# A two-layer recurrent kernel on Trainium2: the first attention gates all its batches in its first half and routes in its third and fifth batch

## The chip, the core and the metric

The kernel runs as one program on one core of a Trainium2 chip. A core has a matrix engine (TensorE, in the rows PE for its multiplications and PEld for its weight loads), a vector engine (VectorE, DVE), a scalar engine (ScalarE, ACT), a general engine (GpSimd, POOL), and SyncE (SP), which here only starts DMAs. The engines run their own instruction streams and meet by semaphores. The metric is the device time of one execution in microseconds (us); the median of three runs of the kernel before is 748.44 us (747.85 to 749.85).

## What is computed

The input x has 8 batches of 512 tokens with 128 features, all float32. Two layers follow each other; in each, a normalised x goes through an attention s and a gated feed-forward part g, and x + s * silu(g) goes on.

```python
xn = _layernorm(x)
s = _L0_attn_ref(xn, W, b)              # causal attention, one head of 128, 512 x 512 scores for each batch
g = _silu(_L0_ffn_ref(xn, ...))         # below
x = x + s * g
xn = _layernorm(x)
s = _L1_attn_ref(xn, Mq, Mk, Mv)        # 8 heads of 64
g = _silu(_L1_ffn_ref(xn, ...))         # top 1 of 8 experts
x = x + s * g
```

```python
def _L0_ffn_ref(x, ...):
    xn = _layernorm(x, ln_g, ln_b)      # a second normalisation, with its own scale and shift
    abel = gelu(xn @ aw1 + ab1) @ aw2 + ab2
    logits = xn @ gate_w + gate_b       # 6 experts
    tw, ti = top_k(logits, 2)           # each token goes to its 2 best experts
    ... nonabel = (weighted sum of the 2 experts' outputs) @ expm(gens[0]) @ ... @ expm(gens[3])
    gate = sigmoid(concat(abel, nonabel) @ gc_w + gc_b)
    return x + abel * (1 - gate) + nonabel * gate
```

## The kernel before, in words

The program has these stages, one after the other:

1. The **first attention** (functions `batch`, L500 on TensorE, L635 on ScalarE, L800 on VectorE), batch by batch, eight times. A batch is 4 tiles of 128 tokens. Everything in it is written out by hand: each engine has one fixed order, with semaphore waits between them. The batch makes q, k and v from `xT` (L515, L517, L521), then for each of 4 query tiles: scores (L528), the largest of each row (L822), the exponential (L646), the turned exponentials (L535, copied by L829), the product with v (L545).
2. The **experts of layer 0**: 74 blocks of 128 rows (two halves of 37), each fetched from a table in DRAM (`x_half`), turned (L1023), sent up (L1033), through a gelu (L1125), down (L1043), and stored (L1358) to `y_half`. Half 0 holds the rows of batches 1 to 4, half 1 those of batches 5 to 8.
3. The dense part of layer 0 and the mixing, while POOL gathers the experts' rows back (L974).
4. Layer 1, attention and experts, to the end of the program.

Beside each batch of the first attention, the engines do other work of layer 0:

- **Normalisation.** VectorE takes mean and variance of a batch (`statistics`, L252), POOL makes the two scales from them (`scales`, L325: six small operations), VectorE writes the normalised tiles (`norm`, L675), POOL multiplies them by the second scale (L365, into `xh`, a part of `pool_xy`). TensorE turns both (`turn_xs` L422, `turn_xh` L429), ScalarE stores them as `xT` and `xn2T`.
- **Gate.** TensorE multiplies `xn2T` by the gate weights (`gate`, L484), VectorE stores the logits (`store_gate`, L704). Batch k prepares batch k + 1: its norm, its turns, its gate.
- **Routing.** After four gated batches VectorE picks each token's two experts (`picks`), TensorE counts (`ranks`), VectorE makes the slots (`offsets`, `first_blocks`, `slots`). This stands in batch 4 and batch 8 (`routes`, L832).
- **Scatters.** POOL writes each tile of `xh` to the rows of `x_half` that the slots name: two indirect DMAs for each of 32 tiles, each followed by a small clear (`spacer`, L350) that it waits for. The order on POOL is fixed: 8 scatters beside each of the preparations of batches 6, 7 and 8, the rest of half 0 after them, half 1 after batch 8's slots, then four additions of a bias (`add_bias`, L340).
- **Rounds.** The exponentials of the four generator matrices take 20 rounds (`exp_round` L436, `store_round` L683): 12 Taylor steps, one turning, 4 squarings (16 matrix instructions in place of 8), 3 products. Two stand in each of batches 1 to 7 and six in batch 8. In batch 8 the expert weights are turned as well (`turn_weights`), and after it they are multiplied by the product of the exponentials (L599, L605). The experts can't start before that (`w_ok`, L1029 and L1212).

## Time and profile before

| what | value |
|---|---|
| median of 3 runs | 748.44 us |
| the profiled execution, its own time | 754.12 us |
| its span, first to last instruction | 752.4 us |
| busy: PE, DVE, POOL, ACT | 641.5, 514.8, 445.5, 397.5 us |
| mean granted clock of TensorE | 0.954 of full |
| first attention, from the first q (L515) to the last product with v | 12.3 to 147.1 us |
| first expert block's first multiplication (L1033) | 158.86 us |

A row of the trace has the start and the length of an instruction or of a merged group in us, then the engine, the line of the kernel, the operation, what it writes and reads, and in brackets how long the engine stood idle before it and what ended that. A row of the windows gives a stretch, its length, the busy time of each engine in it, the granted clock of TensorE (1.00 is 2.4 GHz, 0.50 is 1.2 GHz), the mean share of the DMA engines, and GB/s. A busy TensorE is not TensorE at its peak. Durations come from one execution.

### The profile page before, as it was taken

To read this page: it belongs to the slowest core of one execution; us is meant where nothing else is said; L and a number is where in the kernel's file an instruction comes from. 1 tells how busy PE (TensorE), PEld (TensorE's weight loads), DVE (VectorE), ACT (ScalarE), POOL (GpSimd) and SP (SyncE) were. 2 spreads that over 40 slices of the span, in tenths; PEclk is the share of its full clock that TensorE was granted. 3 is DMA by queue.
4 is the path that set the end of the run, shared out by engine and by line. 5 is a ranking of instruction groups with operands and counts; after the bars stand their busy time and mean duration, and the time that the engine had idled before them with its cause. 6 is when DMAs were issued, how large, how long until landed. Compare 5 with 4: busy or idle time off the path is not lost.

```text
span 752.4 us, 19550 instructions
## 1 busy us (share of the span) xinstructions
PE 641.5 (85%) x6221; PEld 453.7 (60%) x6222; DVE 514.8 (68%) x1349; ACT 397.5 (53%) x1102; POOL 445.5 (59%) x651
## 2 busy tenths in 40 slices
PE   4996869588588888895679999998999999999993
PEld 3775657477587666674425555555999844454442
DVE  5787853947776635898488788786444476777784
ACT  2542442234244344775137767775444376777794
POOL 7441798489818879975016666423333167767692
PEclk9998998979999999997599999999999999999997
DMA  9992001126457631110000000000222101111110
GB/s 255 277 306 79 24 30 40 39 70 138 92 100 137 129 78 35 33 25 15 29 4 25 29 23 26 24 2 13 64 69 70 54 23 37 31 30 30 29 44 15
DMA packets 69466, 48.34 MB, mean 64 GB/s; under 512 B 8011, under 2 KB 63750, under 8 KB 69382
## 3 DMA queue, kind: packets, MB, share of 16 engines
q1 hardware_dynamic: 62332, 34.09, 17.4%
q0 software_dynamic: 6144, 12.63, 7.0%
q8 instruction: 47, 0.77, 0.4%
q10 hardware_dynamic: 906, 0.55, 0.3%
q14 instruction: 37, 0.30, 0.1%
HBM read 24.00 MB, written 23.24 MB: 63 GB/s over the span
## 4 chain that ended last, share of the span: by engine, by line
PE 43%; POOL 21%; issue 15%; DVE 12%; ACT 3%; DMA 3%; SPq 1%; DVEq 1%; POOLq 0%; ACTq 0%
PE bank L1657 9%; PE bank L1616 5%; PE bank L1709 5%; PE bank L1718 4%; POOL pool_xy L974 4%; PE bank L1642 4%; POOL vs L1567 3%; PE bank L1043 3%; PE bank L1033 3%; DMA xg<-x_half 2%; POOL x_half L354 2%; POOL spacer L969 2%; POOL xn_all L1546 2%; ACT pb L1777 1%; PE bank L1023 1%
## 5 line engine op out<-in xcount | busy, mean ns | idle before, releaser
L1777 ACT ACTIVATE pb<-bank,nmx 128x512 f32<-128x512 f32 x256 | 173.0, 689 | 67.0 <-DVE nmx L1908 66.6
L1908 DVE TENSOR_REDUCE nmx<-bank 128x2 f32<-128x1024 f32 x128 | 154.8, 1215 | 6.7 <-PE bank L1657 6.0
L1567 POOL TENSOR_TENSOR vs<-vt,rz 128x256 f32<-128x256 f32 x128 | 78.4, 615 | 118.4 <-DVE rz L1884 114.7
L1657 PE MATMUL bank<-qk 64*128 64x512 f32 x512 | 131.4, 623 | 7.8 <-ACT pb L1777 5.6
L1657 PEld LDWEIGHTS bank<-qk 64*128 64x128 f32 x512 | 42.6, 185 | 63.2 <-ACT pb L1777 32.3
L1125 ACT ACTIVATE turns<-bank,cols 128x128 f32<-128x128 f32 x148 | 46.2, 363 | 65.1 <-PE bank L1033 34.7
L1642 PEld LDWEIGHTS bank<-pb,vs 128*32 128x32 f32 x2048 | 54.2, 110 | 38.0 <-issue 22.4
L354 POOL DMA_INDIRECT x_half<-pool_xy,slot x64 | 62.5, 977 | 19.7 <-issue 10.5
L1642 PE MATMUL bank<-pb,vs 128*32 128x128 f32 x2048 | 69.7, 275 | 2.5 <-POOL vs L1567 2.2
L1777 ACT ACTIVATION_READ_ACCUMULATOR pb<-bank,nmx 128x1 f32 x256 | 53.0, 207 | 0.0
L1596 POOL COPY xn_all<-w 128x512 f32 x39 | 23.9, 613 | 47.8 <-PE bank L1709 47.8
L1033 PE MATMUL bank<-turns 128*128 128x128 f32 x296 | 49.8, 293 | 0.3 <-ACT turns L1125 0.3
L1043 PE MATMUL bank<-w_e,turns 128*128 x296 | 47.3, 284 | 0.8 <-issue 0.8
L1616 PE MATMUL bank<-xn2T,mq 128*32 128x256 f32 x512 | 42.0, 390 | 4.3 <-DVE qk L1860 2.2
L1918 DVE TENSOR_SCALAR xn_all<-bank,cols 128x128 f32<-128x128 f32 x78 | 23.8, 347 | 30.7 <-PE bank L1709 30.7
L974 POOL DMA_INDIRECT yg_first<-y_half,slot x32 | 31.1, 970 | 23.0 <-DMA y_half<-ys 17.8
L1078 PEld LDWEIGHTS bank<-w_a,hid 128*128 128x128 f32 x256 | 33.9, 196 | 16.8 <-issue 12.5
L1023 PE MATMUL bank<-ident,xg 128*128 128x128 f32 x74 | 23.2, 314 | 23.9 <-issue 8.8
L1709 PE MATMUL bank<-xn_all 128*128 128x128 f32 x312 | 43.0, 283 | 0.4 <-ACT xn_all L1787 0.4
L1043 PEld LDWEIGHTS bank<-w_e,turns 128*128 128x128 f32 x296 | 41.2, 201 | 1.0 <-issue 1.0
L1616 PE MATMUL bank<-xn2T,mk 128*32 128x256 f32 x512 | 41.4, 383 | 0.1
L1718 PE MATMUL bank<-w,xn_all 128*128 x312 | 41.4, 276 | 0.1
(254 smaller groups left out, 1387.0 us busy)
## 6 DMA issues: line engine op xcount, KB each, us to landing
y_half<-ys SPq DMA_DIRECT2D x74, 64.5 KB
x_half<-zero SPq DMA_DIRECT2D x2, 2368.0 KB, 21.2
xg<-x_half SPq DMA_DIRECT2D x74, 64.0 KB
x_sorted<-zero SPq DMA_DIRECT2D x1, 2496.0 KB, 19.0
xn_all<-x_sorted SPq DMA_DIRECT2D x39, 64.0 KB, 1.8
y_sorted<-xn_all SPq DMA_DIRECT2D x39, 64.0 KB, 1.6
x_all<-in_L_attn_x_dram SPq DMA_DIRECT2D x8, 256.0 KB, 6.2
w<-in_L_ffn_W_dram SPq DMA_DIRECT2D x1, 2048.0 KB, 11.4
```

The costliest lines, as they stand in the source:

```text
L354: pool.indirect_dma_start(out=x_half[g // NTH], out_offset=bass.IndirectOffsetOnAxis(ap=slot_w[:, g:g + 1], axis=0), in_=xh[:, g, :], in_o ...
L974: pool.indirect_dma_start(out=yg_half[h][:, g % NTH, w, :], out_offset=None, in_=y_half[h], in_offset=bass.IndirectOffsetOnAxis(ap=slot_w[ ...
L1033: mm = pe.matmul(psum[k % 2][:, c * P:(c + 1) * P], wst0[k % NW][:, c * P:(c + 1) * P], xgT0[k % 2][:, :], start=True, stop=True)
L1043: mm = pe.matmul(psum[MBANK[k % 2]][:, 0:DX], hT0[k % NW][:, c * P:(c + 1) * P], w_e2[:, bass.ds(e * EC + c, 1), :].rearrange("p a d -> p ...
L1567: pool.tensor_tensor(vs[s][:, :, :], vt[bt % 2][:, n // 2 % TT, :, :].rearrange("p j d -> p (j d)") .unsqueeze(1).broadcast_to([P, 2, D]), ...
L1616: mm = pe.matmul(bank[j * 32:(j + 1) * 32, i * TH:(i + 1) * TH], w[:, g * KS + j % 2 * 32:g * KS + j % 2 * 32 + 32], xn2T[:, bt * T + j // ...
L1642: mm = pe.matmul(bank[c * 2 * VD:(c + 1) * 2 * VD, at:at + P], vs[k % SLOTS][:, ab, c * 2 * VD:(c + 1) * 2 * VD], pb[k % SLOTS * 2 + ab][: ...
L1657: mm = pe.matmul(psum[score_banks(k) + ab], qk[bt % 2][half, 1, h, 2 * m:2 * m + 2, :].rearrange("p a k -> p (a k)"), qk[bt % 2][half, 0, ...
L1709: mm = pe.matmul(up_part(par, c), wst[par][:, c * P:(c + 1) * P], xgT[par][:, :], start=True, stop=True)
L1718: mm = pe.matmul(psum[(5, 6)[par]][:, 0:D], hT[par][:, c * P:(c + 1) * P], w_2[:, bass.ds(e * HC + c, 1), :].rearrange("p a d -> p (a d)") ...
L1777: act.activation(pb[s + ab][:, :], psum[score_banks(k) + ab], ACT.Exp, bias=nmx[:, s + ab:s + ab + 1], scale=1.0, accum_out=zz[:, s + ab:s ...
L1908: dve.tensor_reduce(nmx[:, s:s + 2], banks[:, score_banks(k):score_banks(k) + 2, :], AX.X, ALU.max, negate=True).then_inc(n_mx, 1)
```

## The change

- **All batches are gated in the first four.** Batch k (k = 1 to 4) now turns `xh` of batches 2k and 2k + 1 and gates batches 2k - 1 and 2k. VectorE's statistics of all batches move to batches 1 to 3, POOL makes all scales by then, and the normalised tiles of batches 3 to 8 are written by ScalarE (`norm`, a scale and a shift, the shift being made by POOL in two more small operations) and not by VectorE.
- **Routing stands in batches 3 and 5**, cut into parts between the steps of the attention: first pick at the batch's start, the other picks after the second and the third tile, the offsets at its end, the slots at the start of the batch behind it.
- **Scatters**: all 64 follow each other on POOL, with their small clears, once the scales and the rows of all batches are done. Each half waits for its own clearing of `x_half`; the clearing of half 0 is issued ahead of the late weights. The four bias additions still stand behind the last scatter.
- **Rounds**: two in batches 1 to 4, then three in each of batches 5 to 8. The turning of the expert weights moves to batches 6, 7 and 8 and its copies to ScalarE; half of the multiplications of the weights moves in front of batch 8's last product.

On POOL in the second half of the first attention stands before (`pool_xy<-xn_all` is a batch's rows by the second scale, `x_half` the scatter, `spacer` its clear; batch 8's preparation, between scatters):

```order
L350 MEMSET spacer 128x384
L354 DMA x_half<-pool_xy,slot 4736x128
L350 MEMSET spacer 128x384
L365 TENSOR_TENSOR pool_xy<-xn_all,rs 128x128 x4
L354 DMA x_half<-pool_xy,slot 4736x128
L350 MEMSET spacer 128x384
```

and now, where batches 7 and 8 are prepared in the first half (`xn_all<-xn_all,ab_bc` is a bias addition):

```order
L359 TENSOR_TENSOR pool_xy<-xn_all,rs 128x128 x4
L366 TENSOR_TENSOR xn_all<-xn_all,ab_bc 128x512
L359 TENSOR_TENSOR pool_xy<-xn_all,rs 128x128 x4
L366 TENSOR_TENSOR xn_all<-xn_all,ab_bc 128x512
L376 DMA x_half<-pool_xy,slot 4736x128
L372 MEMSET spacer 128x384
```

The rows of all batches now stand ahead of the first scatter.

On TensorE in batch 7 stood before (`ident,pool_xy` is the turning of `xh`, `ident,pr` that of the exponentials):

```order
L535 MATMUL bank<-ident,pr 128x128
L528 MATMUL bank<-kT,qT 128x384
L433 MATMUL bank<-ident,pool_xy 128x128 x4
L535 MATMUL bank<-ident,pr 128x128 x2
L545 MATMUL bank<-va,prT 128x128
L528 MATMUL bank<-kT,qT 128x512
```

and now:

```order
L563 MATMUL bank<-ident,pr 128x128
L556 MATMUL bank<-kT,qT 128x384
L563 MATMUL bank<-ident,pr 128x128 x2
L457 MATMUL bank<-gE,gET 128x128 x4
L459 MATMUL bank<-gET,gE 128x128 x4
L486 MATMUL bank<-ident,w_e 128x128 x4
L573 MATMUL bank<-va,prT 128x128
```

The turning of `xh` is gone from it, and a squaring (L457, L459) and a turning of weights (L486) came in.

At the end of batch 8, TensorE had:

```order
L545 MATMUL bank<-va,prT 128x128 x4
L599 MATMUL bank<-rotx,w_e2T 128x129 x12
L605 MATMUL bank<-rotx,eb2T 128x129 x6
L1014 UNCONDITIONAL_BRANCH
```

and has now:

```order
L497 MATMUL bank<-rotx,w_e2T 128x129 x6
L573 MATMUL bank<-va,prT 128x128 x4
L506 MATMUL bank<-rotx,eb2T 128x129 x6
L497 MATMUL bank<-rotx,w_e2T 128x129 x6
L1067 UNCONDITIONAL_BRANCH
```

Six of the twelve multiplications of weights moved ahead of the last product with v.

The diff, cut to its core:

```diff
 # POOL
-            def scales(bt):
+            def scales(j):
...
+                if j > 1:
+                    step(pool.tensor_tensor(nb, mean, r1, ALU.mult))
+                    pool.tensor_scalar(nb, nb, -1.0, None, ALU.mult).then_inc(nb_ok, 1)
...
             scales(0)
+            scale_rows(0)
+            pool.memset(zero[:, :], 0.0).then_inc(t_z, 1)
+            scales(1)
+            scale_rows(1)
+            scales(2)
+            pool.memset(ab2_bc[:, D:DX], 0.0).then_inc(aux_ok, 1)
+            for j in range(2, B):
+                if j + 1 < B:
+                    scales(j + 1)
+                scale_rows(j)
...
+                if j >= B // 2:
+                    add_bias(j - B // 2)
+            for h in range(2):
+                pool.wait_ge(a_sl, h + 1)
+                pool.wait_ge(t_zf[h], 16)
+                for g in range(h * NTH, (h + 1) * NTH):
+                    scatter(g)
             for bt in range(B // 2, B):
                 add_bias(bt)
...
+        ROUNDS = ({1: 0, 8: 1}, {1: 2, 8: 3}, {1: 4, 8: 5}, {1: 6, 8: 7}, {1: 8, 5: 9, 8: 10},
+                  {1: 11, 5: TURNED, 8: SQUARED}, {1: SQUARED + 1, 5: SQUARED + 2, 8: SQUARED + 3},
+                  {1: SQUARED + 4, 3: SQUARED + 5, 5: SQUARED + 6})
+        ROUTES = (2, 4)
 # TensorE, batch
                 scores(2)
-                if bt % (B // 2) == B // 2 - 1:
-                    ranks(bt // (B // 2))
-                if more:
-                    turn_xh(bt + 1, 1 - par)
+                if early:
+                    turn_xh(2 * bt + 1, 0)
                 turn(1)
                 after(5)
+                if bt == 6:
+                    turn_weights(1, bt)
...
                 values(0)
                 scores(3)
+                if bt in ROUTES:
+                    ranks(ROUTES.index(bt))
                 after(7)
+                if bt == 5:
+                    turn_weights(0, bt)
                 turn(2)
                 values(1)
+                if early and 2 * bt + 2 < B:
+                    turn_xh(2 * bt + 2, 0)
                 after(8)
                 turn(3)
...
+                    gate(2 * bt, TT * E0)
+                    gate(2 * bt + 1, 0)
                 values(2)
...
                 if not more:
-                    turn_weights(3)
+                    rotate_weights(0)
+                    rotate_weights(1)
                 values(3)
 # ScalarE, batch
+            def norm(j):
+                act.wait_ge(nb_ok, j - 1)
+                for t in range(TT):
+                    act.activation(xn_all[:, j * TT + t, :], x_all[:, j * TT + t, :], ACT.Identity,
+                                   bias=row_scale(nb1, j, t), scale=row_scale(rs1, j, t)).then_inc(a_xsa, 1)
...
+                if early and bt:
+                    norm(2 * bt + 1)
...
                     if t == 1 and more:
                         store_xT(bt + 1, 1 - par)
+                    if t == 1 and early and 2 * bt + 2 < B:
+                        norm(2 * bt + 2)
                     if t == 2:
...
+                        if early:
+                            store_x2T(2 * bt + 1)
 # VectorE, batch
-                if more:
-                    norm(bt + 1, 1 - par)
-                if bt + 2 < B:
...
+                if bt == 0:
+                    norm(1)
+                if bt - 1 in ROUTES:
+                    slots(ROUTES.index(bt - 1))
+                if bt in ROUTES:
+                    first_pick(ROUTES.index(bt))
+                if bt < 3:
+                    statistics(dve, (2, 5, 7)[bt])
                 after(1)
...
-                if routes:
-                    picks(h)
                 top(0)
                 top(1)
+                if bt in ROUTES:
+                    others(ROUTES.index(bt))
+                if bt < 2:
+                    statistics(dve, (3, 6)[bt])
...
                 top(2)
+                if bt in ROUTES:
+                    second_pick(ROUTES.index(bt))
                 store_turned(1)
...
                 store_turned(2)
+                if bt in ROUTES:
+                    offsets(ROUTES.index(bt))
+                if bt == 0:
+                    statistics(dve, 4)
 # experts of layer 0
-                if k == 1:
-                    pe.wait_ge(w_ok, 6)
+                if k == 0:
+                    pe.wait_ge(w_ok, 4)
```

## Rows read from the trace of the kernel before

**Rows 1.** Windows: batches 1 to 4, 7, 8, and the stretch behind.

```profile
12.30:27.00 14.70, 13.89 (x91) 10.86 (x91) 11.74 (x39) 6.12 (x16) 8.94 (x25) 1.00 0.84 248
27.02:40.09 13.07, 12.26 (x84) 9.68 (x83) 9.87 (x31) 6.25 (x16) 4.86 (x9) 1.00 1.07 329
40.09:53.37 13.28, 12.27 (x85) 9.65 (x83) 11.71 (x41) 6.25 (x16) 6.53 (x14) 1.00 1.06 301
53.37:74.73 21.36, 14.99 (x88) 12.06 (x87) 15.62 (x55) 6.46 (x16) 4.84 (x9) 0.84 0.40 111
...
103.70:124.39 20.69, 15.33 (x89) 12.05 (x87) 7.79 (x21) 6.47 (x16) 18.71 (x29) 0.84 0.13 41
124.39:147.10 22.71, 17.96 (x123) 14.54 (x121) 18.01 (x54) 5.20 (x14) 13.46 (x20) 1.00 0.14 42
147.10:157.66 10.56, 6.00 (x38) 5.77 (x37) 5.14 (x16) 1.47 (x4) 8.34 (x12) 0.84 0.12 36
```

**Rows 2.** Timeline of TensorE: its longest waits in batches 4 and 7.

```profile
63.23 0.47 PE L535 MATMUL bank<-ident,pr 128*128 128x128 f32 x1 [5.10 <-ACT pr L646]
...
114.35 1.12 PE L433 MATMUL bank<-ident,pool_xy 128*128 128x128 f32 x4 [4.65 <-POOL pool_xy L365]
```

**Rows 3.** Windows: two us of batch 7, behind its wait.

```profile
116.00:118.00 2.00, 2.00 (x5) 0.86 (x5) 0.42 (x2) 0.65 (x2) 1.76 (x3) 0.50 0.25 76
```

**Rows 4.** Timeline of the picks in batch 4, VectorE and POOL.

```profile
57.98 1.35 POOL L344 TENSOR_TENSOR xn_all<-xn_all,ab_bc 128x512 f32<-128x512 f32 x1
58.25 1.20 DVE L718 TENSOR_TENSOR tie<-tie,rev 128x96 f32<-128x96 f32 x1
...
60.94 0.26 DVE L718 TENSOR_TENSOR tie<-tie,rev 128x96 f32<-128x96 f32 x1
```

**Rows 5.** Timeline: batch 1's second round; in batch 3 a turning, an exponential, a gate.

```profile
22.03 1.06 PE L440 MATMUL bank<-gE,gAT 128*128 128x128 f32 x8
...
46.59 0.60 PE L433 MATMUL bank<-ident,pool_xy 128*128 128x128 f32 x4
...
47.71 0.58 ACT L646 ACTIVATE pr<-bank,nm 128x384 f32<-128x384 f32 x1 [0.73 <-DVE nm L822]
...
50.91 0.95 PE L488 MATMUL bank<-w_gate,xn2T 128*128 128x6 f32 x8
```

**Rows 6.** Timeline of POOL: rows, first and last of the scales, scatters of half 1.

```profile
26.23 1.47 POOL L365 TENSOR_TENSOR pool_xy<-xn_all,rs 128x128 f32<-128x128 f32 x4 [1.84 <-DVE xn_all L679]
28.36 0.23 POOL L331 TENSOR_SCALAR ve<-mv_st 128x4 f32<-128x4 f32 x1 [0.65 <-DVE mv_st L257]
...
30.74 1.04 POOL L338 TENSOR_TENSOR rs<-ve,half_neg 128x4 f32<-128x4 f32 x1
...
148.49 0.96 POOL L354 DMA_INDIRECT x_half<-pool_xy,slot  x1 [9.15 <-DVE slot L757]
...
197.65 1.02 POOL L354 DMA_INDIRECT x_half<-pool_xy,slot  x1 [0.16 <-issue]
```

**Rows 7.** Groups of lines: ScalarE's like operation in layer 1 (busy, mean ns).

```profile
L1166 ACT ACTIVATE xn_all<-x_all,nb,r 128x128 f32<-128x128 f32 x32 | 13.2, 496 | 5.8 <-DVE nb L1304 5.8
```

**Rows 8.** Timeline of TensorE from the last product with v to the experts.

```profile
145.96 1.16 PE L545 MATMUL bank<-va,prT 128*128 128x128 f32 x8
...
150.40 4.53 PE L599 MATMUL bank<-rotx,w_e2T 128*128 128x129 f32 x24 [3.29 <-DVE rotx L876]
...
158.86 0.68 PE L1033 MATMUL bank<-turns 128*128 128x128 f32 x4
```

**Rows 9.** Windows of the experts: a stretch beside scatters, a stretch without.

```profile
174.60:197.80 23.20, 19.17 (x145) 17.02 (x145) 15.99 (x50) 9.65 (x31) 20.69 (x31) 1.00 0.64 135
208.50:223.40 14.90, 13.45 (x105) 12.00 (x104) 10.32 (x35) 7.13 (x24) 0.03 (x1) 1.00 0.55 99
```

**Rows 10.** Timeline behind the last scatter, VectorE and POOL.

```profile
198.60 5.52 DVE L1219 COPY turns<-w_e 128x256 f32 x1
...
199.05 4.91 POOL L344 TENSOR_TENSOR xn_all<-xn_all,ab_bc 128x512 f32<-128x512 f32 x4
```

More of the change, by code:

```diff
@@ L151, in recurrent_d2_kernel @@
         t_z = sem("t_z")
-        t_zf = sem("t_zf")
+        t_zf = [sem(f"t_zf{i}") for i in range(3)]
         blk = ctx.enter_context(nc.Block())
@@ L261, in _ @@
         def _(dve):
-            for i in range(2):
-                dve.wait_ge(ld_x[i], 16)
-                statistics(dve, i, i, lambda t: x_all[:, i * TT + t, :])
+            for j in range(2):
+                statistics(dve, j)
         first = early.enter_context(ExitStack())
@@ L498, in ranks, with batch @@
                 mm.then_inc(a_rt, 1)
[L500 removed]
+            def batch(bt):
+                par, more, early = bt % 2, bt + 1 < B, bt < EARLY
+                rounds = ROUNDS[bt]
                 def after(i):
[L502 to L509 removed]
+                    if i in rounds:
+                        pe.wait_ge(a_xT, bt + 2 if i == 1 or not more else bt + 3)
+                        exp_round(rounds[i])
                 pe.wait_ge(a_xT, bt + 2)
@@ L865, in batch @@
-                if bt == 1:
-                    weight_sums()
-                if not more:
-                    store_weights(3)
-            for bt in range(B - 2):
-                batch(bt, bt % 2, True, {1: [bt * ROUNDS], 8: [bt * ROUNDS + 1]})
-            last_two(batch)
-            dve.wait_ge(r_ev, G - 1)
-            dve.tensor_tensor(scr[:, 0, :], rot, gc_bc[:, 1, :], ALU.mult).then_inc(r_ev, 1)
-            dve.wait_ge(r_ev, G)
-            dve.tensor_reduce(rotx[:, D:DX], scr[:, 0, :], AX.X, ALU.add).then_inc(r_ev, 1)
```

336 lines of the change are left out of this document (166 added, 170 removed).

## The prediction

> **What bounds the kernel now.** I read first where the change acts: the windows, one for each batch of the first attention [rows 1]. The reader is to see two kinds of batch. Batches 2 and 3 take 13.1 and 13.3 us with TensorE busy for 12.3 of them at the full clock: TensorE sets their length, nearly. Batches 4, 7 and 8 take 21.4, 20.7 and 22.7 us, and the stretch behind them another 10.6 us with TensorE busy for 6.0. The eight batches run from 12.3 to 147.1 us.
>
> The timeline of TensorE says what the long ones wait for [rows 2]. In batch 4 it stands idle for 5.10 us, because VectorE makes all its picks before the first row maximum that ScalarE's exponential needs. In batch 7 it stands idle for 4.65 us for POOL's rows of `xh`, which are queued behind eight scatters. Behind both, the granted clock is 0.50 (1.2 GHz) for a while [rows 3], and the window of the whole batch shows 0.84 where its neighbours show 1.00 [rows 1]. Batch 7 is thus 7.4 us longer than batch 3, of which 4.65 us is the wait and some 2.8 us the lower clock.
>
> Then the seam to the experts [rows 8]: the last product with v ends at 147.1 us, the weights' multiplications start at 150.40 us (VectorE had still the slots of half 1 to make), take 4.53 us, and the first block goes up at 158.86 us: 11.7 us in all.
>
> Behind that, everything follows the experts' start. POOL's gathers wait for the stored blocks, not for its own scatters, so that a shift of the experts is passed on to the end.
>
> **The change, part by part.** I add up each batch in the new order, from 12.3 us (what stands ahead of it is the same). The unit is batch 3, 13.3 us. TensorE's pieces are [rows 5]: turning one `xh` 0.60 us, one Taylor round 1.05 us (a squaring is twice that), one gate 0.95 us.
>
> Batch 1 has the same two gates as before, and one more turning of `xh`, that of batch 3. This is where POOL becomes the bound. A set of scales lasts from 28.36 to 31.78 us, 3.4 us, and with two small operations for the shift 3.9 us; a set of rows is 1.47 us [rows 6]. Before the rows of batch 3, POOL now makes the scales of batches 2, 3 and 4 and the rows of batch 2. Counted from the start of the scales of batch 2 (10.8 us) this is 3.4 + 1.5 + 3.9 + 0.2 + 3.9 us, with the wait for VectorE's statistics of batch 4 some 24.4 us, and the rows are there at 25.9 us. TensorE comes to them ahead of the second round, which began at 22.03 us [rows 5]. So it waits for 4 us, and as after the two waits above I charge 3 us for the lower clock: 14.7 + 4.0 + 3.0 = 21.7 us.
>
> Batch 2 pays a second turning and a second gate: 13.1 + 0.6 + 0.95. ScalarE's norm is not shown in this stage; its like in layer 1 takes 13.2 / 32 = 0.41 us for a tile [rows 7], so 1.65 us for a batch. One norm falls into the idle time ahead of the first exponential, the other in front of the third, where ScalarE stood idle for 0.73 us [rows 5]; most of the rest lies under the additional turning, and I leave 0.5 us: 15.2 us. What the move takes off VectorE (1.3 us a batch) is no gain, as VectorE is busy for 9.9 to 11.7 us of 13 [rows 1].
>
> Batch 3 routes. The twelve operations of the picks, at 0.26 us and a gap each, were one piece of 4.3 us before; now 1.5 us stand at the batch's start, in place of the norm, and 0.9 and 1.2 us between the tiles. These are in the chain from the exponential to the turned copy, and with the offsets (1.2 us) I put 2.6 us on the path, one gate (0.95 us), and 0.5 us for clashes with POOL (below): 17.3 us. Batch 4 has one turning, two gates and the slots, in place of VectorE's norm and statistics, which took as long: 14.2 us.
>
> Batches 5 to 8 have no turning of `xh` and no gate, 1.55 us less. Batch 5 routes again, with a third round: TensorE's 12.8 us would do, but VectorE's chain is as in batch 3, 15.9 us. Batch 6: one turning round and one turning of weights (0.6 us each) and a squaring's second half (1.05 us): 14.0 us. Batch 7 has three squarings and two turnings of weights, 5.4 us more less 1.55: 17.2 us, of which 0.4 us fills TensorE's present gaps: 16.8 us. Batch 8 has three small products (0.4 us) in place of two rounds, no next batch, and the first half of the multiplications of weights (1.4 us): 12.5 us.
>
> The sum is 21.7 + 15.2 + 17.3 + 14.2 + 15.9 + 14.0 + 16.8 + 12.5 = 127.6 us, against 134.8 us before: 7.2 us less. Half of the gain from batches 4, 7 and 8 goes into batch 1.
>
> The seam: behind the last product come six bias multiplications and six of weights, half of [rows 8]'s 24 passes plus 12, at the full clock 2.7 us; a copy (0.5 us) and the semaphores bring the first block up after 3.8 us, not 11.7: 7.9 us less. The first block goes up at 12.3 + 127.6 + 3.8 = 143.7 us, not 158.9.
>
> The experts: nine matrix passes make a block, so 23.2 us beside scatters hold 145 / 9 = 16.1 blocks, 1.44 us each, and 14.9 us without hold 11.7, 1.28 us each [rows 9]. Scatters now start when the rows of batch 8 and the slots are there, near 72.5 us (batch 4's start at 66.5, 4.3 us to ScalarE's last norm, the rows, a bias addition). Half 1's 31 steps took 49.2 us [rows 6], 1.59 each, so 64 take 101 us, to 173.5 us. They overlap the experts for 30 us, before for 40: some 7 blocks gain 0.16 us, 1.1 us. The 38th block, the first to need half 1, comes 37 x 1.44 us and the stall below (4 us) behind the first, near 201 us; there are 27 us in hand. Clearing and late weights only change places on SP's queue; the DMA engines' share falls from 1.06 to 0.40 in batch 4 and is 0.13 in batch 7 [rows 1], so both are in before the first scatter.
>
> One stall stays. While POOL made its four bias additions (4.91 us), one copy of VectorE's, of 256 columns, took 5.52 us, and the blocks stood [rows 10]. These additions are still behind the last scatter, hence still beside the experts. I count no gain for it.
>
> In all 7.2 + 7.9 + 1.1 = 16.2 us. The profiled execution's own 754.12 us would become 737.9 us. The runs' median is 5.7 us below that execution; I take the same difference off the median: 748.44 - 16.2 = **732.2 us**.
>
> **Bounds of what no row shows.** The clock behind batch 1's wait: nothing (behind 3.29 us of idle time the 24 passes at 150.40 us took 0.19 us each, so this is the less likely end) to 3 us. ScalarE's norm in front of the third exponential: 0 to 1.65 us in each of three batches. Picks between the tiles: 0 us on the path to all of their 3.3 us, in two batches. Together they allow from 6 us more gain to 6 us less.
>
> **Rivals.**
> A, *more is saved*: VectorE's statistics come early enough that POOL is ready with TensorE, or the clock holds. Batch 1 costs 15.3 us and the early batches hide the norms; 6 us more, 726 us. For it: POOL is busy for only 8.9 us of batch 1 before [rows 1]. Against it: POOL's chain is serial, and none of its steps can be left out.
>
> B, *the picks clash with POOL*: in batch 4 one small VectorE operation ran beside a POOL addition and took 1.20 us, where its like took 0.26 us [rows 4]. POOL worked for 4.8 us of that batch; in the new batch 3 it works for 12 of 17 us. If nine of the eleven such operations pay 0.94 us, 8.5 us are lost, less the 0.5 us counted: the gain is 8.2 us, 740 us. Against it: four fifths of POOL's pieces are short. The Trainium skill has this as a rule (SBUF — State Buffer, "SBUF: two separate sides"): VectorE and GpSimd share one pair of ports, held exclusively for a whole instruction, by a vector operation with two SBUF inputs against a GpSimd operation that reads SBUF too. By that rule the trace's slow operation and the stalled copy are one thing, and scatters, whose clears read nothing, would not hurt the picks of batch 5.
>
> C, *slower*: the first four batches each wait for POOL or ScalarE in turn (ScalarE's norm needs POOL's shift, POOL's rows need the norm, TensorE needs the rows), and the clock falls in each, as in batch 7. The price is that batch's surplus, 7.4 us, four times: 29.6 us. Without the wait and clock of batch 1 the change saves 23.2 us. So it ends 6.4 us above, 755 us; it decides from 5.8 us for each of the four. For it: POOL's work for a batch pair is 12 us of a 15 us batch. Against it: it is less than the batch, and after batch 1 each set of rows is made about a batch ahead of its use.
>
> D, *nothing moves*: the experts' end is set by POOL, so that a faster attention is given back. For that the scatters must end behind 201 us and they end near 173 us; or the gathers of half 0 (32 steps like the scatters', 51 us) must outlast the blocks of half 1, which take as long. 748 us.
>
> **Chances.** Forecast (728 to 738 us) 0.53; A 0.22; B 0.15; C 0.06; D 0.04. About 0.3% (2.2 us) is what a measurement of this kernel can tell from no change. Forecast, A and B are faster by more: 0.90; D is the same: 0.04; C is slower: 0.06. The range takes in A's lower side and B's upper side: 722 to 743 us.
>
> **What would show it.** Right: in the new profile batches 4 to 8 take 14 to 17 us with no wait of TensorE above 2 us; batch 1 has a wait of 3 to 5 us for POOL's rows with a clock of 0.5 behind it; the experts' first L1033-like multiplication is near 144 us; scatters run without a break from 70 to 174 us; the long VectorE copy beside the four additions is there again, near 175 us; and from there on all is as before, 16 us earlier. Wrong: waits for POOL in batches 2 to 4 (C), small vector operations of 1 us in batch 3 (B), or a distance from first to last expert block above 119 us (D).

## The result, and the profile after

The changed kernel takes 728.73 us (median of 4 runs, 725.46 to 731.12), the kernel before in the same session 748.14 us: a ratio of 0.9745, 95% interval 0.9702 to 0.9788. That is 19.4 us less (16 to 22), where 16.2 us were forecast. The profiled execution has a span of 728.1 us and its own time is 729.79 us.

Windows of the changed kernel, one row for each of batches 1, 3, 4, 7 and 8 and for the stretch behind them (as in [rows 1]: start and end, length, busy time of TensorE, weight loads, VectorE, ScalarE and POOL, the granted clock, DMA share, GB/s):

```profile
12.28:33.12 20.84, 17.31 (x95) 13.36 (x95) 13.89 (x58) 8.32 (x21) 15.35 (x42) 0.92 0.98 273
...
48.23:64.58 16.35, 14.57 (x101) 11.72 (x100) 13.20 (x48) 9.99 (x25) 8.72 (x18) 1.00 0.79 223
64.58:78.56 13.98, 13.15 (x92) 10.57 (x91) 11.18 (x36) 7.80 (x20) 9.98 (x15) 1.00 0.06 20
...
108.88:125.91 17.03, 15.58 (x112) 12.74 (x111) 10.34 (x25) 6.78 (x17) 15.21 (x23) 1.00 0.19 59
125.91:139.40 13.49, 11.14 (x73) 8.62 (x72) 8.01 (x26) 6.16 (x17) 12.17 (x18) 1.00 0.13 40
139.40:143.40 4.00, 2.94 (x27) 2.73 (x26) 2.21 (x5) 1.48 (x4) 3.51 (x6) 1.00 0.18 56
```

Against [rows 1]: the 21.4, 20.7 and 22.7 us of batches 4, 7 and 8 are 14.0, 17.0 and 13.5 us, the 10.6 us behind them (11.7 with the gap to the first block) are 4.0, and the clock is at its full level from batch 2 to the seam. Batch 1 has become 6.1 us longer. Timeline of POOL and TensorE in batch 1 (start, length, engine, line, operation, names and shapes, number; in brackets the idle time before and what ended it):

```profile
24.83 1.47 POOL L359 TENSOR_TENSOR pool_xy<-xn_all,rs 128x128 f32<-128x128 f32 x4
...
26.35 1.12 PE L441 MATMUL bank<-ident,pool_xy 128*128 128x128 f32 x4 [2.38 <-POOL pool_xy L359]
27.26 1.92 PE L448 MATMUL bank<-gE,gAT 128*128 128x128 f32 x8
...
29.78 1.85 PE L514 MATMUL bank<-w_gate,xn2T 128*128 128x6 f32 x16
```

POOL's rows are ready at 26.3 us (forecast 25.9); TensorE waits 2.4 us for them, and the Taylor round behind takes 1.92 us where it took 1.06 at the full clock [rows 5].

Timeline of TensorE at the seam, and of POOL at the first gather of each half:

```profile
138.36 1.06 PE L573 MATMUL bank<-va,prT 128*128 128x128 f32 x8
139.26 1.50 PE L506 MATMUL bank<-rotx,eb2T 128*128 128x129 f32 x12
140.60 1.50 PE L497 MATMUL bank<-rotx,w_e2T 128*128 128x129 f32 x12
...
143.41 0.67 PE L1086 MATMUL bank<-turns 128*128 128x128 f32 x4
```

```profile
204.77 1.04 POOL L1027 DMA_INDIRECT yg_first<-y_half,slot  x1 [27.00 <-DMA y_half<-ys]
...
255.43 0.96 POOL L1027 DMA_INDIRECT pool_xy<-y_half,slot  x1 [0.16 <-issue]
```

No wait of 3.3 us stands in front of the weights' multiplications any more [rows 8], and the first block goes up at 143.41 us, 15.4 us before its place in the kernel before. The second fence becomes important below: half 1's gathers start right behind half 0's, without a wait.

The stall of [rows 10] is there again, as VectorE, POOL and TensorE in the experts:

```profile
170.74 5.59 DVE L1273 COPY turns<-w_e 128x256 f32 x1
...
171.26 4.91 POOL L366 TENSOR_TENSOR xn_all<-xn_all,ab_bc 128x512 f32<-128x512 f32 x4
...
176.99 0.45 PE L1076 MATMUL bank<-ident,xg 128*128 128x128 f32 x1 [4.77 <-DVE turns L1279]
```

### The profile page after: what moved, and what is told of

It reads as the page before. It is cut to its first block, busy times and chain, and to the rows that moved or that the text cites. A ratio compares the mean times of both kernels' runs of the same rounds, so it can differ in the third digit from the quotient of the medians.

```text
span 728.1 us, 19566 instructions
## 1 busy us (share of the span) xinstructions
PE 637.2 (88%) x6221; PEld 449.7 (62%) x6222; DVE 502.3 (69%) x1319; ACT 409.3 (56%) x1132; POOL 447.6 (61%) x663
## 4 chain that ended last, share of the span: by engine, by line
PE 46%; POOL 19%; issue 15%; DVE 10%; DMA 4%; ACT 3%; SPq 1%; DVEq 1%; ACTq 0%; POOLq 0%
PE bank L1712 10%; PE bank L1671 5%; PE bank L1764 5%; PE bank L1773 5%; PE bank L1697 4%; POOL vs L1622 4%; POOL pool_xy L1027 4%; DMA xg<-x_half 3%; POOL xn_all L1600 2%; PE bank L1086 2%; PE bank L1096 2%; PE bank L573 2%; POOL spacer L1022 2%; POOL pool_xy L359 1%; POOL xn_all L1581 1%
## 5 line engine op out<-in xcount | busy, mean ns | idle before, releaser
L376 POOL DMA_INDIRECT x_half<-pool_xy,slot x64 | 62.3, 974 | 10.6 <-issue 10.6
L1973 DVE TENSOR_SCALAR xn_all<-bank,cols 128x128 f32<-128x128 f32 x78 | 23.8, 346 | 30.6 <-PE bank L1764 30.6
L1086 PEld LDWEIGHTS bank<-turns 128*128 128x128 f32 x296 | 40.3, 197 | 0.9 <-DVE turns L1279 0.9
L1848 ACT ACTIVATE xn_all<-bank,cols 128x128 f32<-128x128 f32 x78 | 24.4, 364 | 29.1 <-PE bank L1764 29.1
## 6 DMA issues: line engine op xcount, KB each, us to landing
x_sorted<-zero SPq DMA_DIRECT2D x1, 2496.0 KB, 18.6
```

Source lines behind the costliest of these rows:

```text
L376: pool.indirect_dma_start(out=x_half[g // NTH], out_offset=bass.IndirectOffsetOnAxis(ap=slot_w[:, g:g + 1], axis=0), in_=xh[:, g, :], in_o ...
L1086: mm = pe.matmul(psum[k % 2][:, c * P:(c + 1) * P], wst0[k % NW][:, c * P:(c + 1) * P], xgT0[k % 2][:, :], start=True, stop=True)
```

## The experiments

They ran in three later sessions on three chips, in which the kernel before takes 735.8, 735.7 and 734.1 us, 1.6 to 1.9% under its first time. The first of these sessions has the changed kernel again (716.8 us, 0.9751 of the kernel before) and the variants "rows of batch 3 first", "bias additions between scatters" and "picks in one piece"; the second has the kernel before again, "the same piece behind v", "second routing in batch 8" and "rows first and bias between"; the third has the rest.

Each variant is read as its ratio to the kernel before in its own session. A difference in us to the changed kernel is one of medians in the first session, and in the other two the difference of the ratios times 735 us. Traces are read against the second traces of both kernels. The attention takes the same time there as in the first session (batches 2 to 8 of the changed kernel agree within 0.02 us); from half 1's first gather to the end the changed kernel takes 460.7 us in place of 472.7.

**Both kernels once more.** The changed one:

> The changed kernel once more, as the common base of the next runs and for a second trace. By the prediction's sum it stands 16.2 us under the kernel before, by its first runs 19.4 us (728.7 us). Theory 1: the 19.4 us are the 15.4 us by which the first expert block is earlier and 2 to 4 us of the experts, which come back in this trace: first to last expert block 106 us, as in the first trace. Theory 2: the 7.5 us between the expert stages of the first two traces (113.6 against 106.1 us) are mostly chance of one profiled execution: this trace then shows 108 to 112 us.

Measured: 716.78 us, ratio 0.9751 (0.9717 to 0.9784), 19.0 us less. The kernel before:

> The kernel before once more, for a second trace. Its expert blocks took 113.6 us from first to last in its first trace; in the four traces of the changed kernel and its variants they took 102.3 to 106.1 us. If that is what the change does to the experts, this trace shows 112 to 115 us again; if it is chance of one execution, 105 to 109 us. First block near 156 us either way.

One run, 734.0 us; its trace has 107.6 us from the first to the last expert block's turning, not 113.6. The changed kernel's second trace has 102.6 us, not 106.1, and so neither the 106 us of theory 1 nor the 108 to 112 us of theory 2. TensorE's multiplications of the weights and its first block, and POOL's first gathers, in this second trace of before, then in that of the changed kernel the block and the gathers:

```profile
151.01 2.92 PE L599 MATMUL bank<-rotx,w_e2T 128*128 128x129 f32 x24 [3.28 <-DVE rotx L876]
...
157.86 0.67 PE L1033 MATMUL bank<-turns 128*128 128x128 f32 x4
...
219.39 1.04 POOL L974 DMA_INDIRECT yg_first<-y_half,slot  x1 [13.02 <-DMA y_half<-ys]
...
270.30 0.96 POOL L974 DMA_INDIRECT pool_xy<-y_half,slot  x1 [0.20 <-issue]
```

```profile
143.15 0.67 PE L1086 MATMUL bank<-turns 128*128 128x128 f32 x4
...
203.11 1.13 POOL L1027 DMA_INDIRECT yg_first<-y_half,slot  x1 [25.65 <-DMA y_half<-ys]
...
254.03 0.96 POOL L1027 DMA_INDIRECT pool_xy<-y_half,slot  x1 [0.17 <-issue]
```

The first block is 14.7 us earlier, half 0's gathers 16.3 us and half 1's 16.3 us, where the first pair of traces has 15.4, 18.6 and 22.2 us. So the first execution of before was by chance about 6 us slow, most of it behind its first block (its own time was 5.7 us above the median too), and in the second pair the change is worth 15 us up to the first block and 1.6 us from there to half 0's gathers. That last stretch is 59.1 to 63.9 us in the six traces that have the changed kernel's order from the seam on, so that 1.6 us by itself is not told from nothing. In both of these traces half 1's gathers start 50.9 us behind half 0's.

**Rows of batch 3 before the scales of batch 4.**

```diff
             for j in range(2, B):
+                if j == 2:
+                    scale_rows(j)
                 if j + 1 < B:
                     scales(j + 1)
-                scale_rows(j)
+                if j > 2:
+                    scale_rows(j)
```

> POOL makes the rows of batch 3 before the scales of batch 4, and not behind them; nothing else changes. Theory (the prediction's step on batch 1): TensorE's wait of 2.4 us for these rows and the half clock behind it go away; batch 1 falls from 20.8 to about 16.3 us and the kernel to about 724 us, 4 to 5 us under the changed kernel. Rival 1: the clock falls for another reason: only the wait goes, 2.4 us, 726 us. Rival 2: the scales of batch 4 and 5 come late, and ScalarE's norms in batch 2 wait for them: nothing is gained, 728 to 729 us, and batch 2 is longer than 15.1 us by what batch 1 saves.

Measured: 712.52 us, 0.9689 (0.9656 to 0.9721), 4.3 us under the changed kernel. Batch 1:

```profile
12.04:27.28 15.24, 14.09 (x95) 11.17 (x95) 13.55 (x58) 8.21 (x21) 13.24 (x36) 1.00 1.02 295
```

It is 5.6 us shorter than with the wait (15.2 us, 16.3 expected), and batch 2 is as before (15.1 us). The theory holds, and the slowest of the six runs (715.86 us) is under the fastest of the changed kernel's (716.20); only POOL's order made the wait.

How much of it is the clock? The two next variants leave batch 1 alone and have the same wait. In them the rows behind it read (from the run with whole picks):

```profile
25.21 0.66 PE L441 MATMUL bank<-ident,pool_xy 128*128 128x128 f32 x4 [2.37 <-POOL pool_xy L359]
25.71 1.06 PE L448 MATMUL bank<-gE,gAT 128*128 128x128 f32 x8
```

The round takes 1.06 us: the clock held, and batch 1 took 18.3 us in place of 20.8. Of the six traces in which the wait is 2.4 us (this code stands in all), the round took 1.92 us in three and 1.06 us in three. Where the clock held, the batch ends 5.2 us behind the end of the wait. Where it fell, it ends 6.8 us behind it in both traces of the changed kernel, and 9.7 us behind it in the run with the second routing in batch 8 (window of that run, from the end of the wait to batch 2):

```profile
25.51:35.22 9.71, 9.71 (x46) 9.71 (x47) 2.94 (x13) 1.40 (x3) 4.15 (x14) 0.51 0.90 257
```

So behind the same wait the low clock costs nothing, 1.6 us or 4.5 us. Up to 0.9 us more go at the first q and k, where the traces differ too. Which of these comes was not controlled in any run; the wait is always paid.

**Bias additions one by one between scatters.**

```diff
+            BIAS_AFTER = (5, 8, 11, 17)
...
                 for g in range(h * NTH, (h + 1) * NTH):
                     scatter(g)
-            for bt in range(B // 2, B):
-                add_bias(bt)
+                    if g in BIAS_AFTER:
+                        add_bias(B // 2 + BIAS_AFTER.index(g))
```

> The four bias additions that stood together behind the last scatter stand one by one between scatters (behind the 6th, 9th, 12th and 18th tile), beside the attention; nothing else changes. Theory: the stop of the experts goes, in which one copy of VectorE took 5.6 us beside the four additions and TensorE waited 4.8 us; scatters end 5 us later (176 us), which costs three to four blocks 0.16 us each; batches 5 to 8 pay up to 1 us in all. 4 us less, 724 to 725 us. Rival 1: each addition holds up a small operation of VectorE in the attention by up to 1.2 us and the four together cost as much there: 728 to 729 us. Rival 2: a copy of VectorE in the experts then waits for the scaling of mq (1.5 us), which comes behind the last scatter in any case: 1.3 us of the gain are lost, 726 us.

Measured: 710.08 us, 0.966 (0.9621 to 0.9699), 6.7 us under the changed kernel, more than the 4 us of the theory; in its trace batch 1 was 2.6 us shorter by the clock. From the first block's start to the first gather it is 56.2 us, not 60.0, and batches 5 to 7 take 14.6, 15.4 and 17.0 us as without the additions. Beside the first of them:

```profile
86.59 1.28 POOL L366 TENSOR_TENSOR xn_all<-xn_all,ab_bc 128x512 f32<-128x512 f32 x1
86.72 0.15 DVE L893 RECIPROCAL rz<-z 128x1 f32<-128x1 f32 x1
86.79 0.34 DVE L801 TENSOR_TENSOR_SCAN run<-reset,bank 128x96 f32<-128x96 f32 x1
87.16 0.25 DVE L802 TENSOR_TENSOR off<-run,bank 128x96 f32<-128x96 f32 x1
```

No operation of VectorE is longer than elsewhere: these read a bank of PSUM, or one small operand. The next two additions stand beside like operations or an idle VectorE (the one at 107.86 us), the last beside like ones again. The scaling of `mq` (a weight of layer 1, which POOL scales behind the last scatter) still cost little (the copy beside it took 0.66 us, its like 0.28).

**Picks in one piece, at the batch's start.**

```diff
                 if bt in ROUTES:
                     first_pick(ROUTES.index(bt))
+                    others(ROUTES.index(bt))
+                    second_pick(ROUTES.index(bt))
...
-                if bt in ROUTES:
-                    others(ROUTES.index(bt))
...
-                if bt in ROUTES:
-                    second_pick(ROUTES.index(bt))
```

> Both routings are made in one piece at the start of batches 3 and 5, as the kernel before made them, and not in three parts; nothing else changes. Theory (the prediction's step on batch 3): all 4.3 us of the picks then stand ahead of the first row maximum, TensorE waits 3 to 5 us in each of the two batches and its clock falls behind it: each batch 3 to 6 us longer, the kernel 735 to 740 us. Rival: the parts between the tiles cost as much on the path as the piece at the start, and the split buys nothing: 728 to 730 us. In between: a wait of 3 us without a fall of the clock, 734 us.

Measured: 715.98 us, 0.9733 (0.9691 to 0.9774): no difference. Batch 3 takes 16.3 us (16.3 with parts), batch 5 14.5 us (15.0). My theory falls: against one piece ahead of v, cutting buys nothing. A new one was that the place counts, ahead of v or behind it.

**The same piece behind v**, where the kernel before has it (diff against the run before this one):

```diff
-                if bt in ROUTES:
-                    first_pick(ROUTES.index(bt))
-                    others(ROUTES.index(bt))
-                    second_pick(ROUTES.index(bt))
                 if bt < 3:
                     statistics(dve, (2, 5, 7)[bt])
                 after(1)
...
+                if bt in ROUTES:
+                    first_pick(ROUTES.index(bt))
+                    others(ROUTES.index(bt))
+                    second_pick(ROUTES.index(bt))
                 top(0)
```

> Both routings in one piece, as in the run before this one, but behind v and in front of the first row maximum, which is where the kernel before had them; batches 3 and 5 as before otherwise. Theory (new): not the cutting matters but the place: ahead of v VectorE waits for TensorE anyway, behind v the whole 4.3 us are on TensorE's path. Batches 3 and 5 take 3.5 to 4.5 us more each, plus up to 2 us each for the clock; the kernel 7 to 12 us above the changed kernel, 0.985 to 0.992 of the kernel before. Rival (the prediction's rule, that one piece costs and parts do not) says the same here, and is already contradicted by the piece at the start that cost nothing. Rival 2: even here it costs nothing (0.975), and the long wait in the kernel before was due to something else of its batch 4, such as the slow operation beside POOL.

Measured: 726.77 us, 0.988 (0.9837 to 0.9922), 9.5 us above the changed kernel: half of what the whole change gains. Batches 3 and 5 take 20.5 and 19.2 us, 9.0 us more in all than in the run before this one. Batch 3, VectorE and TensorE:

```profile
49.16 0.69 DVE L872 TENSOR_TENSOR va<-bank,bv_bc 128x512 f32<-128x512 f32 x1
...
49.76 0.24 DVE L770 TENSOR_REDUCE m<-lg_all 128x16 f32<-128x96 f32 x1
50.04 1.36 DVE L771 TENSOR_TENSOR tie<-lg_all,m 128x96 f32<-128x96 f32 x1
...
54.66 0.29 DVE L882 TENSOR_REDUCE nm<-bank 128x1 f32<-128x128 f32 x1
...
55.50 0.47 PE L563 MATMUL bank<-ident,pr 128*128 128x128 f32 x1 [5.29 <-ACT pr L687]
```

The wait of 5.1 us of [rows 2] is back as 5.29 us. (The 1.36 us pick started at 50.04 beside a bias addition of POOL at 50.03: the 1.20 us of [rows 4] again.) With the same piece ahead of v (the run before this one) the picks run while TensorE makes q, k, the round and v, 4 us in which VectorE has nothing else that is urgent, and that wait is 0.96 us. In the changed kernel the first pick alone stands there; the other picks, some 2 us a batch, stand behind v between the tiles, and batches 5 and 6 are 0.5 and 0.7 us longer than with the whole piece ahead of v. A cut with all its parts behind v was not run, so whether parts help in that place is open.

**The kernel before, with its picks ahead of v alone.**

```diff
+                routes = bt % (B // 2) == B // 2 - 1
+                h = bt // (B // 2)
+                if routes:
+                    picks(h)
                 after(1)
                 dve.wait_ge(a_qkv, bt * 3 + 3)
...
-                if routes:
-                    picks(h)
                 top(0)
```

> The kernel before with one edit: its picks (in one piece, in batches 4 and 8) stand ahead of the Taylor round and v, behind the norm and the statistics, and not behind v. Theory (place): in batch 8, which has neither norm nor statistics at its start, the picks then lie wholly beside TensorE's products (3.0 us of wait gone); in batch 4 VectorE is busy with norm and statistics until 54.5 us of the first trace, so that the picks end near 59 us, 2 to 3 us earlier than before, and the first row maximum comes that much earlier; the clock may stay up behind the shorter wait. 5 to 9 us less, 0.988 to 0.993. Rival: the position among the steps gives nothing by itself, since the round and v wait behind the picks instead: 0.998 to 1.001.

Measured: 725.93 us, 0.9898 (0.9866 to 0.9931), 7.5 us less by the ratio for four moved lines. Batch 4 takes 16.6 us (21.6 in the second trace of before), batch 8 and the seam 30.6 (33.7). TensorE in batch 4:

```profile
59.85 0.65 PE L426 MATMUL bank<-ident,xn_all 128*128 128x128 f32 x4 [0.97 <-DVE gE L686]
...
61.47 0.33 PE L535 MATMUL bank<-ident,pr 128*128 128x128 f32 x1 [0.97 <-ACT pr L646]
```

The 5 us of batch 4 are more than the 2 to 3 expected: the idle time of 5.1 us is now two waits of 0.97 us, and the clock stayed up.

**The second routing in batch 8 again.**

```diff
-        ROUTES = (2, 4)
+        ROUTES = (2, 7)
...
             for bt in range(B):
                 batch(bt)
+            slots(1)
```

> The second routing stands in batch 8 again, with its slots behind the last batch, as in the kernel before; all else is as in the changed kernel. Half 1's scatters then start behind the slots, near 143 us, and end near 194 us, the bias additions near 199 us. Theory (the prediction's step on the seam): VectorE's slots (3.5 us) stand in front of its first expert work, and the picks and offsets lie in batch 8, where TensorE has least to do: the first block comes 3 to 5 us later; the scatters lie beside the experts for 50 us and not 30, 0.16 us for each of 14 blocks, 2 us; 5 to 7 us above the changed kernel, 0.982 to 0.985 of before. Rival 1: the seam's gain came from the weights' multiplications and the clock, not from the routing: the first block comes less than 1.5 us later, 0.977 to 0.979. Rival 2: POOL sets the end here: gathers of half 0 start later than 5 us after those of the changed kernel (relative to the first block).

(The diff shown leaves out two further waits of TensorE.) Measured: 718.13 us, 0.977 (0.9726 to 0.9813), not told apart from the changed kernel. Batch 8 and the seam to the first block's start are 20.0 us, not 17.3, but batches 5 and 6 are 13.3 and 14.4, not 15.0 and 15.3: a routing costs some 2.5 us in either place. The early second routing gains 2.7 us at the seam and costs 2.5 us in batches 5 and 6, so that the first block is no earlier for it; that it comes 2.5 us later in this trace is the clock of batch 1 (23.2 us for 20.8). From the first block to the first gather there are 61.8 us for 60.0: this fits some 2 us for scatters beside the experts for 50 us and not 30, but lies within the spread given above.

**The kernel before, with all scatters behind the last rows.**

```diff
-                if bt == 5:
-                    pool.wait_ge(a_sl, 1)
-                    pool.wait_ge(t_zf, 16 * 3)
-                if bt >= 5:
-                    for g in range((bt - 5) * TT, (bt - 4) * TT):
-                        scatter(g)
-            for g in range(3 * TT, NTH):
+            pool.wait_ge(a_sl, 1)
+            pool.wait_ge(t_zf, 16 * 3)
+            for g in range(NTH):
                 scatter(g)
```

> The kernel before with one edit: no scatter until the rows of all batches are made; then all 64 in a row. Theory: the wait of TensorE for POOL's rows in batch 7 (4.65 us) and the low clock behind it (2.8 us) go, so that the first expert block comes 7 us earlier, near 151 us; but the scatters begin near 118 us and end near 220 us, the bias additions and the scaling of mq behind them near 227 us, and the gathers of half 0 behind those, 4 to 8 us later than before: 1.005 to 1.011 in all. The part of the change that takes the wait away is then of use only with the gating of all batches in the first four, which lets the scatters start at 70 us. Rival: POOL's end is not what the gathers wait for, and the 7 us reach the end: 0.990.

Measured: 732.65 us, 0.9983 (0.9967 to 0.9998). Batch 7 in the second trace of before, then here:

```profile
104.03:123.98 19.95, 14.59 (x88) 11.32 (x87) 7.78 (x21) 6.47 (x16) 18.13 (x28) 0.83 0.12 39
```

```profile
102.86:116.30 13.44, 12.73 (x89) 10.13 (x87) 7.69 (x21) 6.26 (x16) 12.02 (x18) 1.00 0.11 35
```

The wait and the low clock are gone, and batch 6 is shorter by 1.1 us; the last product with v ends 8.8 us earlier. But the first expert block waits 8.43 us:

```profile
152.56 0.96 POOL L354 DMA_INDIRECT x_half<-pool_xy,slot  x1 [0.17 <-issue]
...
156.66 0.47 PE L1019 MATMUL bank<-ident,xg 128*128 128x128 f32 x1 [8.43 <-DMA xg<-x_half]
```

This is half 0's last scatter; it ends at 153.5 us (they began at 103.7, since the rows are done sooner than I assumed), and no block of half 0 can load before it has landed. The result lies between both of my theories, and both named the wrong place: what the attention gained, the first block gave back (its first multiplication at 157.98 us, for 157.86). This is what the gating in the first four batches is for: scatters from 70 us, and no rows queued behind them.

**Norms on VectorE again** (ScalarE's `norm` calls are removed):

```diff
 # VectorE, batch
+                if 0 < bt < EARLY:
+                    norm(2 * bt + 1)
                 if bt < 3:
                     statistics(dve, (2, 5, 7)[bt])
...
                 top(1)
+                if bt < EARLY - 1:
+                    norm(2 * bt + 2)
```

> The changed kernel with the norms of batches 3 to 8 on VectorE again (at the places at which ScalarE makes them), 1.2 us each; the rest as changed. Theory: in batches 2 and 4 VectorE has room and nothing is lost (the prediction's step); in batch 3, where picks, norm and statistics meet at the start (1.5 + 1.2 + 1.3 us), the first row maximum comes 1 to 1.5 us late, and a second norm stands between the tiles, 1.2 us on the path: the kernel 1 to 4 us above the changed kernel, 0.977 to 0.980. Rival 1: VectorE is the engine that now sets the length of the first four batches: 1.2 us for each of six norms, 7 us, 0.985. Rival 2: nothing or a gain, as VectorE's norm is shorter than ScalarE's (1.2 against 1.64 us) and POOL's rows come earlier: 0.972 to 0.975.

Measured: 720.86 us, 0.9821 (0.9784 to 0.9859), five runs from 715 to 722 and one of 727. Batches 2, 3 and 4 take 15.8, 17.2 and 15.2 us, 2.7 us more in all than on ScalarE. The theory's size fits the trace; by the ratio the kernel is 5.1 us up, and its interval only just meets the changed kernel's.

**Rows first and bias between, together.**

> Rows of batch 3 ahead of the scales of batch 4, and the four bias additions one by one between scatters: the two edits that gained 0.6% and 0.9% of the kernel before when made alone. Theory: they act in different places (batch 1, and the experts' stop), so they add up: 0.960 of the kernel before, 11 us under the changed kernel. Rival: both work through the start of half 0's gathers, behind which POOL's chain of 64 gathers (50.7 us) sets when half 1's can start, but half 1's blocks are nearly as late: when the gathers start 9 us earlier, the blocks become the limit and 2 to 4 us are given back: 0.964.

Measured: 708.39 us, 0.9636 (0.9595 to 0.9677). It gains 8.5 us over the changed kernel, where the single ones gained 4.3 and 6.7; the intervals of all three overlap, so that the sum is not shown by the times. The trace has it: batch 1 is 5.3 us shorter than in the changed kernel's second trace, the stretch from the first block to the first gather 3.0 us, together 8.3. The 11 us of the theory counted batch 1's clock twice, since the bias run's trace had 2.6 us of its gain there. The rival's account does not fit: half 1's gathers start 51.0 us behind half 0's, as ever, and right behind them (0.29 us idle), so that the blocks gave nothing back.

**And without the small clears behind half 0's gathers.**

```diff
-                    space()
+                    if g >= NTH:
+                        space()
```

> Rows of batch 3 first and bias additions between the scatters (as in the run with both), and in addition no small clear behind the gathers of half 0. Theory: in all traces so far half 1's gathers start 50.6 to 51.0 us behind those of half 0 (64 steps of 1.59 us, of which 0.6 us are the clear and its gap), while the last block is stored 0 to 2 us before: POOL sets the rest. Without the clears the 64 steps take some 40 us or less, and half 1's gathers start when the last block is stored: 0 to 2 us earlier, 0.961 to 0.9636. Rival 1: it is slower, since 64 gathers without gaps crowd the DMA engines and half 1's blocks wait longer for their rows (xg): 0.966 or more. Rival 2: more than 2 us are gained, since the clears hold up VectorE's copies in half 1's blocks: 0.960 or less.

Measured: 703.27 us, 0.9592 (0.9566 to 0.9617), the best of all: 1.6% (11.7 us) under the changed kernel. Against the run with both it is 3.2 us by the ratios, with intervals that overlap. POOL's end of half 0 and start of half 1:

```profile
231.37 0.95 POOL L1031 DMA_INDIRECT yg_first<-y_half,slot  x1 [0.31 <-issue]
240.56 0.95 POOL L1031 DMA_INDIRECT pool_xy<-y_half,slot  x1 [8.24 <-DMA y_half<-ys]
```

A half has 32 gathers, not the 64 that I wrote: at 1.26 us each, not 1.59, they take 40 us, and then POOL waits 8.24 us for the last stored block. The blocks set the start of half 1's gathers now, 48.3 us behind half 0's and not 51.0, which is 2.7 us, somewhat above the theory's 0 to 2. (Another 2.8 us between the two traces lie ahead of the first gather, where the kernels are the same.) Besides, VectorE's copies of the weights are shorter without clears beside them. The group of that copy in the gathers' stretch (busy, mean ns), with clears and without:

```profile
L1277 DVE COPY turns<-w_e 128x256 f32 x29 | 11.7, 404 | 0.1
```

```profile
L1278 DVE COPY turns<-w_e 128x256 f32 x30 | 9.7, 322 | 0.1
```

## Why the prediction was right, and where its reasons were not

- **The sum.** Forecast 16.2 us; measured 19.4 and 19.0 us with intervals that reach down to 16. The second pair of traces shows 16.3 us up to the gathers (17.6 us in the whole span). The excess of the first pair of traces (24.3 us) was mostly the slow first execution of before. Of the signs named, the wait of 3 to 5 us in batch 1 did not come (2.4 us); no wait of TensorE in batches 4 to 8 is above 1.5 us, and the scatters run from 70.6 to 170.9 us.
- **The batches.** Forecast 21.7, 15.2, 17.3, 14.2, 15.9, 14.0, 16.8, 12.5 us; in the trace 20.8, 15.1, 16.4, 14.0, 15.0, 15.4, 17.0, 13.5: 127.1 for 127.6 in all. The routed batches were 0.9 us shorter each, batches 6 and 8 1.4 and 1.0 longer. That the sum comes out within 0.5 us is in part luck: terms too high by 3.0 us and too low by 2.6 us cancel. Batch 6 lacked a term: VectorE makes the slots of half 1 at its start, and with the second routing in batch 8 it takes 14.4 us.
- **Batch 1.** The mechanism was right (POOL's scales in front of its rows), the terms mis-sized: the wait is 2.4 us, not 4.0, as TensorE came at 24.0 us and not 22.0; the clock behind it costs nothing, 1.6 or 4.5 us, so that the 3 us charged lie within what comes but describe no execution. Both are avoidable by POOL's order, at no price that the trace shows.
- **The routing.** This step failed in its reason: "now 1.5 us stand at the batch's start" was credited to the cutting. Whole picks at the start cost nothing more than parts, whole picks behind v cost 9.5 us. What the kernel before paid in batch 4 was the place.
- **The rows of `xh`.** Right: 6.5 us in batch 7, isolated by the run with late scatters. What the prediction did not see is that in the kernel before this wait cannot be taken away alone: the first block then waits for half 0's last scatter.
- **The seam.** 4.0 us for 3.8 forecast. Whether the weights' 24 passes ran at the low clock before was chance too: behind the same wait of 3.3 us they took 4.53 us in the first trace of before, 4.41 and 4.52 us in its two variants, and 2.92 us in the second trace of before. The removal of the second routing from batch 8 is no part of the net gain. How the rest divides among rounds, the turning of weights and the halves of the multiplications was not tried.
- **The experts.** 1.1 us forecast, 3.1 and 1.6 us measured in two pairs, between executions that differ by up to 4.8 us in this stretch: not shown.
- **Rival A** was half right: POOL could be ready in time, but not in this order.
- **Rival B** did not come: in batch 3 the slowest of the picks took 0.45 us and one copy of the offsets 0.75. The rule of the Trainium skill (SBUF — State Buffer, "SBUF: two separate sides"), as the prediction gives it, fits the two slow picks (1.20 and 1.36 us): they have two inputs in SBUF, beside an addition that reads SBUF. It fits the picks of batch 5 too, which stand beside scatters and clears and take 0.25 or 0.26 us each. The copy of 5.6 us has one input only; for it the section has another case, a vector operation in a two-port mode, and it counts copies among those that can have one. By the section whoever starts first holds the pair for its own instruction. This trace does not bear that out: the copy's row begins 0.5 us ahead of the first addition and ends behind the fourth.
- **Rival C** did not come: TensorE waits for POOL's rows by less than 1 us in every batch after the first.
- **Rival D.** Its second mechanism (gathers of half 0 outlast half 1's blocks) is real, but small: in every trace but the first of before, POOL was idle for less than 0.5 us before half 1's gathers, until the clears went. Where that gather waits for the last block, it starts 2.6 us behind the start of that block's store; in the others 2.9 to 5.7 us. So POOL holds the end up by 0 to 3 us (an estimate from these rows).

## What to carry to other kernels

An off-path chain on an in-order engine belongs where that engine would wait anyway for another one's product; move it there before cutting it into pieces, since the place gave 7.5 us in one kernel and 9.5 in the other, and the cutting nothing on top of it. When a producer's queue holds both the work that someone waits for and work for later (POOL's scales and rows, additions behind scatters), order it by who waits first: two such reorderings were worth 8.5 us. And ask of each transfer chain what starts behind its last piece: a removed wait brought the end of the attention 8.8 us forward and the kernel's end at most 2.4 us, because half 0's scatters had not ended.

## What was not expected of the hardware

- After the same wait of 2.4 us in the same code, TensorE's clock was halved in three executions, at a cost of 1.6, 1.6 and 4.5 us, and full in three. A dip seen in one trace is not a price; the wait is.
- One copy of VectorE took as long as four additions of POOL in a row (5.6 us for 4.9), though each addition is an instruction of its own; one by one, beside operations on PSUM or an idle VectorE, the same four cost nothing that the trace shows.
- With a clear of 0.45 us on POOL behind each gather, VectorE's copies took 404 ns in the mean, without it 322 ns (some 30 copies of one trace each).
